# Mamba scan in a fused four-block kernel: product with B by ScalarE and TensorE transposes in two of five steps

## What is computed

```
delta = softplus(dt @ dt_proj_w.T + dt_proj_b)
A = -exp(A_log)
def step(h, inp):
    u_t, d_t, B_t, C_t = inp
    dA = exp(d_t[..., None] * A)
    h = dA * h + (d_t * u_t)[..., None] * B_t[:, None, :]
    y = einsum('bdn,bn->bd', h, C_t)
    return (h, y)
```

## Time and profile before

| | |
|---|---|
| median of 3 runs | 1072.91 us (1071.75 to 1073.18) |
| the profiled execution's own time | 1076.65 us |
| its span in the profile | 1074.6 us |
| VectorE busy | 871.7 us (81%) |
| TensorE busy (matmuls) | 824.9 us (77%) |
| GpSimd busy | 656.0 us (61%) |
| ScalarE busy | 440.2 us (41%) |
| mean granted clock of TensorE | 0.90 of full speed |

### The profile page before, as it was taken

The page is one execution under the profiler, slowest core; times in us unless marked ns, Lnnn a source line. Parts: engine busy times, 40 slices in busy tenths (PEclk is TensorE's granted clock), DMA queues, the critical chain, the costliest instruction groups (busy, mean ns, idle before and its releaser), DMA issues.

```text
span 1074.6 us, 6964 instructions
## 1 busy us (share of the span) xinstructions
PE 824.9 (77%) x2210; PEld 379.4 (35%) x2210; DVE 871.7 (81%) x672; ACT 440.2 (41%) x501; POOL 656.0 (61%) x294
## 2 busy tenths in 40 slices
PE   3977998976387877789885999897637787778835
PEld 2433443432133423244443444343213242334414
DVE  5999885479988999999897488547998899999830
ACT  3734331158545333455364423214843423345212
POOL 2446993111699797888361499311169979889810
PEclk8987999988689999999997999998968899999966
DMA  3000000003445564555000100000224555555401
GB/s 96 1 0 0 0 0 1 0 5 107 103 147 192 179 207 176 178 184 167 1 0 3 17 0 0 1 0 5 93 79 138 194 190 195 182 191 193 145 0 20
DMA packets 37808, 91.05 MB, mean 85 GB/s; under 512 B 16264, under 2 KB 16400, under 8 KB 37776
## 3 DMA queue, kind: packets, MB, share of 16 engines
q1 hardware_dynamic: 37456, 89.62, 25.2%
q0 software_dynamic: 320, 1.05, 0.4%
HBM read 87.51 MB, written 3.15 MB: 84 GB/s over the span
## 4 chain that ended last, share of the span: by engine, by line
DVE 39%; PE 32%; POOL 14%; issue 9%; ACT 5%; DMA 1%; SPq 0%; POOLq 0%; DVEq 0%; ACTq 0%
DVE arena L1416 10%; POOL arena L319 9%; PE ps L650 9%; PE ps L446 7%; DVE ps L1410 5%; PE ps L545 4%; ACT arena L754 4%; DVE arena L1371 3%; PE ps L644 3%; DVE arena L1273 3%; POOL arena L327 2%; PE ps L452 2%; POOL arena L312 1%; PE ps L591 1%; PE ps L435 1%
## 5 line engine op out<-in xcount | busy, mean ns | idle before, releaser
L319 POOL TENSOR_TENSOR arena<-arena 128x1024 f32<-128x1024 f32 x128 | 302.5, 2376 | 66.9 <-DVE arena L1416 40.1
L545 PE MATMUL ps<-arena,mat 128*128 128x512 f32 x512 | 270.2, 654 | 69.4 <-POOL arena L319 58.0
L1416 DVE TENSOR_TENSOR_SCAN arena<-arena,ps 128x1024 f32<-128x1024 f32 x96 | 219.5, 2287 | 20.1 <-POOL arena L319 17.2
L754 ACT ACTIVATE arena<-arena,Amat 128x1024 f32<-128x1024 f32 x96 | 109.9, 1148 | 170.6 <-DVE arena L1416 149.3
L545 PEld LDWEIGHTS ps<-arena,mat 128*128 128x128 f32 x512 | 100.6, 205 | 185.0 <-POOL arena L319 98.3
L754 ACT ACTIVATE arena<-arena 128x1024 f32<-128x1024 f32 (+4 forms) x124 | 80.7, 689 | 134.8 <-DVE arena L1339 74.8
L1410 DVE TENSOR_TENSOR ps<-arena,ps 128x1024 f32<-128x1024 f32 x96 | 116.2, 1210 | 4.8 <-PE ps L535 2.7
L650 PE MATMUL ps<-arena,mat 128*128 128x512 f32 x240 | 106.3, 592 | 0.0
L535 PE MATMUL ps<-arena,sel 96*128 96x512 bf16 x192 | 62.2, 409 | 54.5 <-DVE arena L1416 54.1
L446 PE MATMUL ps<-arena,diag 128*128 128x512 f32 x192 | 87.3, 614 | 2.1 <-ACT arena L754 2.1
L327 POOL TENSOR_TENSOR arena<-arena,BB 128x1024 f32<-128x1024 f32 x32 | 75.3, 2354 | 0.0
(11 more groups left out here) (167 smaller groups left out, 1331.5 us busy)
## 6 DMA issues: line engine op xcount, KB each, us to landing
arena<-bc_rows SPq DMA_DIRECT2D x128, 512.0 KB, 4.1
BB<-bc_rows SPq DMA_DIRECT2D x32, 512.0 KB, 4.9
out<-arena SPq DMA_DIRECT2D x32, 64.0 KB, 2.2
xres<-x POOLq DMA_DIRECT2D x4, 256.0 KB, 5.2
bc_rows<-arena SPq DMA_DIRECT2D x8, 128.0 KB, 2.0
xres<-x SPq DMA_DIRECT2D x4, 256.0 KB, 4.4
convw<-conv_w SPq DMA_DIRECT2D x1, 576.0 KB
mat<-mats SPq DMA_DIRECT2D x1, 448.0 KB, 3.5
```

Of the source, the lines that this page charges most:

```text
L319: tt(HC[s % 2], HS[s % 2], CB[s % 4], ALU.mult).then_inc(S("hc"), 1)
L545: last = mm(half(PS[3], n), ident, half(HC[s % 2], n), start=first, stop=True, skip_group_check=True)
L754: return nc.scalar.activation(out_, in_, func, bias=bias, scale=scale, accum_out=accum_out)
L1416: nc.vector.tensor_tensor_scan(HS[q], a, b, 0.0, ALU.mult, ALU.add).then_inc(S("scan"), 1)
```

## The change

Three things are moved. First, GpSimd's product with B serves every fifth step from 8 on (`Y_STEPS`, s % 5 == 3: 12 per half, before 16). Second, a new kind of step (`X_STEPS`, s % 5 in (1, 4) from 9 on: 22 per half) has no product on VectorE. For it delta*u of an image is transposed once by TensorE (`turn_du`), so that pixels stand on the partitions in 8 blocks of 128 x 128, and copied to SBUF by ScalarE (`keep_du`); the B rows of all four images are transposed as well (`turn_rows`, `keep_b`), so that B of a pixel is one number per partition. In each such step ScalarE scales the 8 blocks by 8 columns (`scaled_input`, 128 x 128 each, into one of two tiles TB), and TensorE transposes them back into the PSUM tile that the scan reads (`turn_scaled`). Third, the 30 other steps (`Z_STEPS`) stay with broadcast and VectorE's product.

To make room, the B and C rows that go to DRAM stand in one tile ROWS, several semaphores are merged, the first product of GpSimd ahead of the loop is gone, and work on PS[2] moves to other steps: the next half's x from 5 to 7, its second part from 13 to 15, skip(0) from 21 to 32 and the first output projection from 22 to 33.

```diff
@@ -112,9 +112,10 @@
             d = D[k]
-            d["BCS32"] = d["BCS"]
             d["BCS"] = d["BCS"].bitcast(bf16)
+            d["HI32"] = d["HI"]
             d["HI"] = d["HI"].bitcast(bf16)
+            d["END"] = arena[:, sum(n for _, n in later):][:, 0:BANK]
 
@@ -130,6 +131,9 @@
         DBP, BB = D[0]["R1"], sb("BB", L)[:, :]
+        ROWS = sb("ROWS", L)[:, :]
+        TB = [ROWS, D[1]["R1"]]
+        BT = D[0]["HI32"].rearrange("p (k j n) -> p k j n", k=BLK, n=D_STATE)
         CB = [D[0]["W2"], D[0]["W3"], D[1]["W0"], D[1]["W1"]]
@@ -153,16 +157,25 @@
         SCANS = 4 * D_STATE
-        BY_POOL = SCANS // 4
-
-        def by_pool(s):
-            return s % 4 == 3
-
-        def row_fill(s):
-            return s - s // 4 + 1
+        Y_STEPS = [s for s in range(SCANS) if s % 5 == 3 and s >= 8]
+        X_STEPS = [s for s in range(SCANS) if s % 5 in (1, 4) and s >= 9]
+        Z_STEPS = [s for s in range(SCANS) if s not in Y_STEPS + X_STEPS]
+
+        def fills(s):
+            return sum(1 for r in Z_STEPS + X_STEPS if r <= s)
 
         def rows_f32(j):
-            return D[j // 2]["R1" if j % 2 else "BCS32"][96:128, :]
+            return ROWS[32 * j:32 * j + 32, :]
+
+        def du_block(j, n):
+            if j % 2 == 0:
+                return blk(D[1]["W4"], n)
+            return blk(D[n // 4]["END"], n % 4)
+
+        def turned(h, j):
+            return 5 * h + [1, 3, 4, 5][j]
+
+        ROWS_TURNED = 2
 
...
@@ -399,18 +414,15 @@
                 plain(pool)
-                pool.wait_ge(S("rows1"), 32 * h + 16)
-                pool.wait_ge(S("du"), 4 * h + 1)
-                input_times_b(h, 3)
                 for s in range(SCANS):
                     state_times_c(h, s)
-                    if by_pool(s) and s + 4 < SCANS:
-                        input_times_b(h, s + 4)
+                    if s + 5 in Y_STEPS:
+                        input_times_b(h, s + 5)
                     if s == 5:
                         delta_u(h, 2 + s // 16)
-                    if h + 1 < HALVES and s in (13, 21):
+                    if h + 1 < HALVES and s in (15, 23):
                         root(A[s // 16], h + 1, 0, s // 16)
@@ -528,12 +540,31 @@
             def b_rows(h, s):
-                if s < SCANS and not by_pool(s):
-                    if s >= 2:
-                        pe.wait_ge(S("scan"), SCANS * h + s - 1)
-                    for n in range(2):
-                        last = mm(half(PS[s % 2], n), blk(sel, s % D_STATE), half(two_images(s // D_STATE, "BCS"), n)[0:96, :], start=True, stop=True)
-                    last.then_inc(S("bb"), 1)
+                if s >= 2:
+                    pe.wait_ge(S("scan"), SCANS * h + s - 1)
+                for n in range(2):
+                    last = mm(half(PS[s % 2], n), blk(sel, s % D_STATE), half(two_images(s // D_STATE, "BCS"), n)[0:96, :], start=True, stop=True)
+                last.then_inc(S("bb"), 1)
+
+            def turn_scaled(h, s):
+                i = X_STEPS.index(s)
+                pe.wait_ge(S("scaled"), len(X_STEPS) * h + i + 1)
+                pe.wait_ge(S("scan"), SCANS * h + s - 1)
+                transposes(TB[i % 2], PS[s % 2]).then_inc(S("bb"), 1)
+
+            def fill(h, s):
+                if s in Z_STEPS:
+                    b_rows(h, s)
+                if s in X_STEPS:
+                    turn_scaled(h, s)
+
+            def turn_du(h, j):
+                pe.wait_ge(S("du"), 4 * h + j + 1)
+                transposes(two_images(j, "DU"), PS[2]).then_inc(S("turned"), 1)
+
+            def turn_rows(h):
+                pe.wait_ge(S("kept"), turned(h, 0))
+                transposes(ROWS, PS[2]).then_inc(S("turned"), 1)
 
@@ -690,28 +721,41 @@
                         plain(pe)
-                    b_rows(h, s + 2)
+                    fill(h, s + 2)
                     sum_of(h, s - 1)
+                    if s == 2:
+                        pe.wait_ge(S("rx1"), 2 * h + 2)
+                        turn_du(h, 0)
+                    if s == 3:
+                        turn_rows(h)
+                    if s == 5:
+                        pe.wait_ge(S("kept"), 5 * h + ROWS_TURNED)
+                        turn_du(h, 1)
+                    if s == 23:
+                        if h + 1 < HALVES:
+                            pe.wait_ge(S("group1"), g_var(h + 1, 0))
+                        else:
+                            pe.wait_ge(S("kept"), turned(h, 1))
+                        turn_du(h, 2)
+                    if s == 28:
+                        pe.wait_ge(S("kept"), turned(h, 2))
+                        turn_du(h, 3)
+                    if s == 32:
+                        pe.wait_ge(S("kept"), turned(h, 3))
+                        skip(0)
                     if h + 1 < HALVES:
-                        if s == 5:
-                            pe.wait_ge(S("rx1"), 2 * h + 2)
+                        if s == 7:
+                            pe.wait_ge(S("kept"), turned(h, 1))
                             x_channels(h + 1, 0, PS[2])
-                        if s == 10:
+                        if s == 12:
                             group_mean(A[0], h + 1, 0, 0)
-                        if s == 13:
+                        if s == 15:
                             pe.wait_ge(S("a_x"), 2 * h + 3)
                             x_channels(h + 1, 1, PS[2])
-                        if s == 18:
+                        if s == 20:
                             group_mean(A[1], h + 1, 0, 1)
-                        if s == 21:
-                            pe.wait_ge(S("a_x"), 2 * h + 4)
-                            pe.wait_ge(S("group1"), g_var(h + 1, 0))
-                            skip(0)
-                    elif s == 21:
-                        pe.wait_ge(S("rx1"), 2 * h + 2)
-                        skip(0)
-                    if s == 22:
+                    if s == 33:
                         out_proj(h, 0)
...
@@ -881,12 +925,48 @@
                     j, q = s // D_STATE, s % 2
-                    act.wait_ge(S("delta"), 4 * h + j + 1)
+                    if s % D_STATE == 0:
+                        act.wait_ge(S("delta"), 4 * h + j + 1)
                     if s >= 2:
                         act.wait_ge(S("scan"), SCANS * h + s - 1)
-                    plain(act)
-                    dst = PS[q][:, :] if by_pool(s) else DA[q]
+                    if s % D_STATE == 0:
+                        plain(act)
+                    dst = PS[q][:, :] if s in Y_STEPS else DA[q]
                     av(dst, two_images(j, "DL"), ACT.Exp, Amat[:, s % D_STATE:s % D_STATE + 1]).then_inc(S("da"), 1)
+
+            def keep_du(h, j):
+                act.wait_ge(S("turned"), turned(h, j))
+                if j >= 2:
+                    act.wait_ge(S("scaled"), len(X_STEPS) * h + sum(1 for s in X_STEPS if s < D_STATE * (j - 1)))
+                if j == 0:
+                    act.wait_ge(S("delta"), 4 * h + 3)
+                    av(D[1]["W4"], PS[2][:, :], ACT.Identity).then_inc(S("kept"), 1)
+                elif j == 2:
+                    av(D[1]["W4"], PS[2][:, :], ACT.Identity).then_inc(S("kept"), 1)
+                else:
+                    av(D[0]["END"], half(PS[2], 0), ACT.Identity)
+                    av(D[1]["END"], half(PS[2], 1), ACT.Identity).then_inc(S("kept"), 1)
+
+            def keep_b(h):
+                act.wait_ge(S("turned"), 5 * h + ROWS_TURNED)
+                act.wait_ge(S("bcs0"), ONE + 2 * h + 2)
+                ps = PS[2][:, :].rearrange("p (k j n) -> p k j n", k=BLK, n=2 * D_STATE)
+                av(BT, ps[:, :, :, 0:D_STATE], ACT.Identity).then_inc(S("kept"), 1)
+
+            def scaled_input(h, s):
+                i, j = X_STEPS.index(s), s // D_STATE
+                if i == 0:
+                    for r in range(2):
+                        act.wait_ge(S(f"rows{r}"), 32 * h + 32)
+                if i == 1:
+                    act.wait_ge(S("bcs1"), ONE + 4 * h + 4)
+                if i > 1:
+                    act.wait_ge(S("bb"), fills(SCANS) * h + fills(X_STEPS[i - 2]))
+                if i == 0 or X_STEPS[i - 1] // D_STATE < j:
+                    act.wait_ge(S("kept"), turned(h, j) if i else 5 * h + ROWS_TURNED)
+                for n in range(BLK):
+                    last = av(blk(TB[i % 2], n), du_block(j, n), ACT.Identity, BT[:, n, j, s % D_STATE:s % D_STATE + 1])
+                last.then_inc(S("scaled"), 1)
 
@@ -1086,15 +1166,26 @@
                         hi_rows(h, 1)
+                        keep_du(h, 0)
+                    if s == 5:
+                        keep_b(h)
+                    if s + 3 in X_STEPS:
+                        scaled_input(h, s + 3)
+                    if s == 7:
+                        keep_du(h, 1)
+                    if s == 25:
+                        keep_du(h, 2)
+                    if s == 30:
+                        keep_du(h, 3)
...
@@ -1402,14 +1493,15 @@
```

(11 more changed lines are left out.)

52 lines of the change are left out of this document (27 added, 25 removed).

## The result

The changed kernel took **1078.1 us** (median of 5 runs, 1077.75 to 1080.04) against 1073.15 for the kernel before on the same chip (5 runs, 1071.75 to 1076.55): ratio 1.0046, 95% interval 1.0027 to 1.0066. It is slower by 0.5%, where 1071 and a small gain were forecast; the range, 1054 to 1088, holds it. The profiled execution took 1078.1 us too, its span is 1076.3.

A forecast was written before the change was run, and what follows sets the result against it. No engine alone was taken to bound; a chain through in-order queues, 15.82 us per five steps, would turn most VectorE savings into waiting. 2 x (0.5 - 1.5) = -2.0 us gave about 1071 us median, range 1054 to 1088.

The forecast's parts named there:

- The chain of 15.82 us: Waits through VectorE's scans, TensorE's transposes and sum, and GpSimd's products: 15.82 us per five steps, 3.16 a step.
- B: Rival: the queues alone bound the scan loop, 13.86 us per group of five steps, total 1033 us; chance 0.04.
- D: Rival: ScalarE's batch of scalings passes 3.6 us, making scans 0.4 us late in 24 groups, total 1084; chance 0.08.
- E: Rival: eight transposes run one after another, 2.4 us, 1.5 more than taken in 24 groups, total 1107; chance 0.03.
- A: Rival: TensorE's sum is off the chain, so a group of five steps takes 15.2 us, total 1057; chance 0.2.
- C: Rival: TensorE's clock slows the sum of step 1 behind the transposes, 1.3 us per group hit, 1083; chance 0.2.
- the term of the 47 steps: Scan 16 to scan 63 in each half: 165.5 us against a mean of 165.1 before, +0.5 per half.
- start, scan 2 to 16: Stretch up to scan 16, bound by GpSimd: about 2 us of waits go, ScalarE's extra work about 0.5 late; -1.5 per half.
- the gate at 0: Gates at steps 33 and 49 stand where VectorE idles anyway, so they were priced at 0.
- Gate and delta: Side work behind scan 17: 4.45 us, part of it hidden by scan 18; +3.5 on average per half.
- The centring's stretch: Centring behind scan 36 was priced at 5.1 us, with its scaling behind a ScalarE batch; layer root at step 38, 2.9.
- The 2.3 for what was not seen: Allowance in the 47 steps of each half for unseen waits: two thirds of the smaller remainder before, 3.4 us.

The follow-up runs named there:

- e1: Changed kernel with GpSimd's product with B moved one state product later; 1067.0 us, ratio 0.9934 to the kernel before.
- e2: Changed kernel with TensorE's sum of step 1 made ahead of the transposes for step 4 in each group; 1069.2 us, ratio 0.9949.
- e9: Changed kernel with seven of the eight transposes of each new step's input left out; 1066.85 us, ratio 0.9919.
- e8: Changed kernel with seven of the eight ScalarE scalings of each batch left out; 1075.2 us, ratio 1.0006.
- e5: Changed kernel with skip and first output projection back at 28 and 29, turning of delta*u of block 3 at 41; 1093.65 us, ratio 1.0180.
- e6: Changed kernel with the third image's output projection behind the sum of scan 63 instead of at step 60; 1076.4 us, ratio 1.0022.
- e7_by_group: Changed kernel with the later product with B and the sum ahead of the transposes, each only in chosen groups; 1056.3 us, ratio 0.9834.

## Why the prediction was wrong, step by step

Right was the mechanism of the undisturbed group. The chain of 15.82 us held in every link, the queue of GpSimd did not bound, and the freed 41.5 us of VectorE became waits; moving or removing a link shortened the group (e1, e2, e9), removing ScalarE's work did not (e8). Rivals B, D and E fell by that: the batch takes 2.43 us, and eight transposes 1.04. A's 15.2 came only once a link was taken away. C, TensorE at 1.2 GHz on the chain, did not come in the undisturbed groups, whose sums took 1.88 us, but it did come in the others.

Wrong was the sum, by terms of one or two microseconds, with a forecast gain of two. The step that failed is the term of the 47 steps, +0.5 per half, which kept every sum of TensorE at its 1.88 us and left the slower clock to rival C at 0.2. Measured were +0.9 and +5.1. Against the first profile of before:

| term, both halves | forecast | measured |
|---|---|---|
| scan 0 to scan 2 | 0 | -1.8 |
| start, scan 2 to 16 | -3.0 | -4.3 |
| 47 steps | +1.0 | +6.1 |
| S(63) to the second half's S(0); last scan to last gate | 0 | +1.6 and +1.4 |
| the end, and ahead of the loops | 0 | -1.6 and +0.4 |
| sum (before rounding) | -2.0 | +1.7 |

- **The clock in the 47 steps.** Windows of the changed kernel, S(36) to S(41) in the first half, then S(36) to S(41), S(41) to S(46), S(46) to S(51) and S(51) to S(56) in the second:

```profile
core 0: us, PE busy (x) PEld busy (x) DVE busy (x) ACT busy (x) POOL busy (x), PEclk, DMA share, GB/s
407.30:431.01 23.71, 15.68 (x63) 8.06 (x61) 18.29 (x11) 11.79 (x24) 17.04 (x8) 0.98 0.38 131
917.88:943.06 25.18, 16.96 (x63) 9.28 (x61) 18.28 (x12) 11.82 (x24) 17.05 (x8) 0.91 0.37 124
943.06:960.28 17.22, 16.90 (x53) 8.45 (x53) 13.69 (x8) 11.57 (x22) 14.00 (x7) 0.84 0.54 183
960.28:979.67 19.39, 15.10 (x45) 6.85 (x46) 16.75 (x9) 12.27 (x29) 14.00 (x7) 0.91 0.44 163
979.67:995.64 15.97, 14.96 (x74) 9.38 (x73) 13.69 (x8) 13.40 (x27) 14.55 (x8) 1.00 0.60 199
```

Timeline inside the fourth of them, with the sum of step 46, h(48) and the gate of step 49:

```profile
968.09 1.06 PE L447 MATMUL ps<-mat,ROWS 128*128 128x128 f32 x8 [3.61 <-DVE arena L1508]
...
968.99 3.40 PE L576 MATMUL ps<-arena,mat 128*128 128x512 f32 x4
...
972.56 2.35 POOL L333 TENSOR_TENSOR arena<-arena 128x1024 f32<-128x1024 f32 x1 [2.17 <-PE ps L576]
...
974.76 1.23 DVE L1512 TENSOR_TENSOR arena<-ps,arena 128x1024 f32<-128x1024 f32 x1 [1.95 <-PE ps L576]
```

TensorE had been idle for 3.61 us; behind the transposes the sum took 3.40 us for 1.88 (3.38 in the first half), and h(48) waits for it. This is C's place in the group and C's price, 1.5 us where it had 1.3, and by estimate most of the 1.95 us that the gate waits, since the gate needs the sum next to that one. The forecast had put the gate at 0, since VectorE idles there anyway, and S(46) to S(51) took 19.40 for 17.7. In S(36) to S(41) the clock parts the halves, 23.71 us at a mean of 0.98 and 25.18 at 0.91. In e9 the first half is the longer one, 24.63 at 0.93 against 22.99 at 0.99, and in e1 23.09 at 0.93 against 21.38 at 1.00. In the kernel before, the same steps took 20.86 us at 1.00 and 20.85 at 0.92, so there the slow stretch cost nothing: the chain did not bind. In S(41) to S(46), 17.2 us for 15.8, two sums in a row took 6.5 us (3.60 at 2.4 GHz); which part of the 1.4 is the clock's is not shown. An estimate from these figures is 4.5 us over both halves, and up to 7 with S(41) to S(46), where the sum was 5 us short.

- **The rest of the 47 steps: 165.5 forecast, 167.4 and 168.8 measured.** The group's 0.14 makes 1.3. The output projection moved from 22 to 33 was given no cost, since the centring's sums "have time", and cost 1.0 us in S(31) to S(36), 16.96 for 15.82 (e5). Gate and delta cost 2.8 for 3.5. The centring's stretch was 23.8 by the sum and 23.7 in the half at 0.98; in it the wait for ScalarE was 1.27, not 2.5, since the sums ahead came 1.16 late. The 2.3 for what was not seen had room for part of this. The common fault: side work was added to VectorE's side of the chain, and not to the in-order TensorE, whose queue and clock the chain also runs through.
- **The tail after the last scan** had no term in the sum, so 0. The gates came 1.5 and 1.4 us later, the skip and projection at step 60 holding up the sum behind h(62) (e6). At the program's end e6 gives it back; between the loops it gives back 0.1 of the 1.6, so that there the cause stays open.
- **The median.** The forecast carried before's distance of 3.7 us between profiled execution and median over to the changed kernel, which had none. Of the 5.0 us between the medians the traces show 1.7; the other 3.3 come from setting a slow execution of one kernel against a median one of the other. Of the 7.1 us between 1071 and the measured median, 3.7 are this step and 3.4 the sum.
- **The chances.** 0.09 for a slower outcome of the forecast's own chain was too small: its terms had errors of several microseconds around a gain of two. C at 0.2 asked for "four sum records over 3 us at h(3) in several groups"; one such group came in each half, and slow stretches beside it. That the time still fell in the range is in part luck: the start and the end were 1.3 and 1.6 us shorter than the sum had them.

## What to carry to other kernels

When engines are coupled step by step, follow the chain through every in-order queue before pricing work that is taken off one of them; here 41.5 us less on VectorE bought nothing until two instructions changed places. Look also at TensorE's granted clock in each stretch, not only its mean: a slow stretch was free while another engine bound (20.85 us at 0.92), and cost 1.5 us once TensorE stood on the chain. Then look where each order helps: the same move gained in undisturbed groups and lost where side work stood in the queue, and chosen by group it gave 2%. A gain of 0.2% that is a difference of terms of 1 to 5 us is no forecast of a sign.

## What was not expected of the hardware

Scan 0 to scan 2 became 0.9 us shorter in each half by one instruction whose work is the same. Timeline of VectorE and GpSimd, before and after:

```profile
282.59 5.64 POOL L319 TENSOR_TENSOR arena<-arena 128x1024 f32<-128x1024 f32 x2
283.90 2.13 DVE L1382 TENSOR_TENSOR arena<-arena 32x1024 bf16<-32x1024 f32 x1
```

```profile
284.25 1.22 DVE L1473 TENSOR_TENSOR arena<-arena 32x1024 bf16<-32x1024 f32 x1
284.30 3.37 POOL L333 TENSOR_TENSOR arena<-arena 128x1024 f32<-128x1024 f32 x1 [1.30 <-DVE arena L1508]
...
285.50 3.25 DVE L1492 TENSOR_TENSOR arena<-arena 128x1024 f32<-128x1024 f32 x1
```

When a GpSimd product was already running, VectorE's subtraction took 2.13 us; when it started 0.05 ahead of the product, 1.22. The product then took 3.37 us instead of 2.35, beside the subtraction and the sum that follows it (L1492, 128 x 1024, both operands in SBUF, 3.25). The rows look like taking turns: the sum ends 1.08 us behind the product's end (287.67), and in the kernel before the subtraction ends 1.08 behind the end of the first product (284.95, its start plus 2.36). The Trainium skill, GPSIMD Engine Reference, section 1. Specifications, has the SBUF interfaces shared with VectorE, with contention for instructions with two SBUF inputs; the rows agree. No run here tried it alone, so that it is a reading of two places.

The stretch between the two loops, the same code in all kernels but for its first microseconds, took from 280.8 us (before) to 284.8 (e7_by_group); in the 51 us that start 7 us behind the last scan the granted clock was 0.97 in the changed kernel (282.4 us in all) and 0.93 in e7_by_group. What sets this is open.
